# A convolution with per-image weights: the sums of an image read from PSUM by VectorE, its small steps gathered there, and the first eight pairs laid out anew

## The reference

```
x1 = group_norm(x)              # 32 groups of two neighbouring channels, eps 1e-5
pooled = x1.mean(pixels)
a = relu(fc1_w pooled + fc1_b)  # 4 values
att = softmax(fc2_w a + fc2_b)  # 4 values
agg_w = sum_k att[k] * weight[k]     # [64 out, 64 in, 3, 3] for each image
agg_b = att @ bias
out = x + conv3x3(x1, agg_w, pad 1) + agg_b
```

## Time and profile before

| | us |
|---|---|
| median of 3 runs | 323.28 (321.74 to 324.62) |
| the profiled execution | 323.93 |
| its span | 322.1 |
| TensorE busy | 301.2 |
| VectorE busy | 215.6 |
| ScalarE busy | 198.2 |
| GpSimd busy | 75.4 |
| mean granted clock of TensorE | 0.973 |

### The profile page before, as it was taken

The page is one execution under the profiler, slowest core; times in us unless marked ns, Lnnn a source line. Parts: engine busy times, 40 slices in busy tenths (PEclk is TensorE's granted clock), DMA queues, the critical chain, the costliest instruction groups (busy, mean ns, idle before and its releaser), DMA issues.

```text
span 322.1 us, 15578 instructions
## 1 busy us (share of the span) xinstructions
PE 301.2 (94%) x7038; PEld 265.2 (82%) x7038; DVE 215.6 (67%) x505; ACT 198.2 (62%) x260; POOL 75.4 (23%) x268
## 2 busy tenths in 40 slices
PE   7289877999899999999999999999999999999994
PEld 5157756988679999988999899967998799988883
DVE  2899584979569494948769494949678594719000
ACT  1090776786484849567684849486675849395321
POOL 1008266028310405040220404050311305000000
PEclk9769995999999999999999999999999999999999
DMA  7962306738392947648292947668392607051464
GB/s 260 421 268 65 141 2 150 254 86 286 77 275 93 228 177 176 227 112 288 51 258 111 239 166 184 218 136 273 84 293 56 180 2 205 2 147 60 118 171 119
DMA packets 16690, 53.61 MB, mean 166 GB/s; under 512 B 7280, under 2 KB 10352, under 8 KB 14704
## 3 DMA queue, kind: packets, MB, share of 16 engines
q1 hardware_dynamic: 16320, 52.40, 54.1%
q10 hardware_dynamic: 304, 0.22, 0.3%
HBM read 26.89 MB, written 25.69 MB: 163 GB/s over the span
## 4 chain that ended last, share of the span: by engine, by line
PE 82%; DVE 8%; POOL 4%; DMA 2%; issue 2%; ACT 0%; SPq 0%; POOLq 0%; DVEq 0%
PE acc L674 82%; DMA x<-x 2%; DVE stats L321 2%; DVE mix L402 2%; POOL var L285 1%; DVE wparts L337 1%; POOL vsum L281 1%; PE tiny L643 0%; DVE wl L446 0%; POOL root L286 0%; DVE mix L400 0%; DVE mv L329 0%; SPq L205 0%; POOL newton L287 0%; DVE o L511 0%
## 5 line engine op out<-in xcount | busy, mean ns | idle before, releaser
L581 ACT ACTIVATE o<-acc,out_par 128x392 f32<-128x392 f32 x127 | 78.9, 670 | 78.8 <-PE acc L674 78.4
L674 PE MATMUL acc<-xl,wh 64*64 64x385 f16 (+3 forms) x2304 | 119.8, 330 | 1.4 <-issue 1.4
L674 PE MATMUL acc<-xh,wh 64*64 64x385 f16 (+3 forms) x2304 | 118.1, 326 | 1.2 <-ACT wh L550 0.5
L674 PE MATMUL acc<-xh,wl 64*64 64x385 f16 (+3 forms) x2304 | 117.4, 325 | 0.6 <-issue 0.6
L674 PEld LDWEIGHTS acc<-xl,wh 64*64 64x64 f16 x2304 | 94.4, 109 | 11.4 <-issue 1.8
L674 PEld LDWEIGHTS acc<-xh,wl 64*64 64x64 f16 x2304 | 91.3, 107 | 11.3 <-issue 1.1
L674 PEld LDWEIGHTS acc<-xh,wh 64*64 64x64 f16 x2304 | 90.8, 108 | 11.9 <-ACT xh L532 0.9
L321 DVE BATCH_NORM_STATS2 stats<-x 128x6 f32<-128x448 f32 x112 | 60.8, 612 | 6.1 <-DMA x<-x 6.1
L455 DVE TENSOR_TENSOR xl<-x,xh 128x1568 f16<-128x1568 f32 x31 | 55.3, 1785 | 0.8 <-ACT x L520 0.8
L520 ACT ACTIVATE x<-x,xof,xsc 128x1568 f32<-128x1568 f32 x32 | 53.8, 1686 | 0.4
L527 ACT ACTIVATE xh<-x 128x1568 f16<-128x1568 f32 x28 | 42.0, 1502 | 0.4
(11 more groups left out here) (71 smaller groups left out, 146.3 us busy)
## 6 DMA issues: line engine op xcount, KB each, us to landing
x<-x SPq DMA_DIRECT2D x15, 1568.0 KB, 9.8
out<-o SPq DMA_DIRECT2D x30, 392.0 KB, 4.5
out<-o SPq DMA_DIRECT2D x30, 294.0 KB, 4.1
out<-o SPq DMA_DIRECT2D x44, 98.0 KB, 2.8
w_sb<-w_t SPq DMA_DIRECT2D x2, 576.0 KB, 8.7
out_par<-par SPq DMA_DIRECT2D x64, 0.5 KB, 2.1
x<-x SPq DMA_DIRECT2D x1, 896.0 KB, 7.1
x<-x SPq DMA_DIRECT2D x1, 448.0 KB, 3.7
```

Source lines behind the costliest of these rows:

```text
L581: nc.scalar.activation(o_sb[i][m][:, g * GN:(g + 1) * GN], acc[n % SLOTS][m][:, 0:GN], ACT.Identity, bias=out_par[i][m][:, 1:2], scale=out ...
L674: ins = nc.tensor.matmul(pixels[:, top:bottom, left:right], weights[i][halves[m], tap * C:(tap + 1) * C], window, start=start and step == ...
```

## The change

- Small steps. The group statistics of every pair run on VectorE (`group_stats` replaces `first_group_stats`, `first_scales` and GpSimd's chain). GpSimd keeps the root; a chunk of the next pair's statistics stands behind it on VectorE.
- Sums. `hidden`, the copies to `hid`, goes. VectorE reads `tiny` itself, which alternates between two banks by pair. The sums are asked for one pair ahead (not two), at places listed in `SUMS_AT`.
- Weights in another order. The second image's partitions hold the four sets as 2, 3, 0, 1, with bias and fc2 to match. So the first two sets of either half cover all four, and the largest is taken over one whole set and two halves of another.
- x in halves. x of pair 0 comes in five pieces, the weights are issued when the second has landed, x of pairs 1 to 3 when the first weights have; later x tiles come in two DMAs, on either side of `spread_params`. xh is made straight from x, in quarters for pairs 0 to 3 and in halves later; x is normalised afterwards. In pairs 1 to 7 VectorE normalises the first half.
- Orders. Pairs 0 to 3 mix, convert and multiply the weights in three parts of three taps. GpSimd makes the second low half of pairs 0 to 3. Pairs 0 to 7 take three groups by kind, then the fourth. The steps of `params` stand between those of the mixture. In pair 0 ScalarE makes the first share of two parts. The warming products are 36, 6 and 9.

The diff, cut to its core:

```diff
-TAP_ORDERS = ((4, 0, 1, 2, 3, 5, 6, 7, 8), (4, 6, 7, 8, 3, 5, 0, 1, 2))
+TAP_ORDERS = ((4, 3, 5, 0, 1, 2, 6, 7, 8), (4, 3, 5, 6, 7, 8, 0, 1, 2))
-PIECES = ((0, 1), (1, 3), (3, 7))
+PIECES = ((0, 1), (1, 3), (3, 5), (5, 6), (6, 7))
-WARM_PRODUCTS = (36, 10, 12)
-FIRST_TAPS = 5
+TURNED = (2, 3, 0, 1)
+WARM_PRODUCTS = (36, 6, 9)
+EARLY = 4
+GROUPED = 8
+SUMS_AT = ((1, 2, 3), (1, 2, 0), (1, 2, 0), (1, 2, 0), (1, 0, 6), (1, 0, 0), (0, 2, 6), (0, 2, 4), (0, 1, 0))
+SUMS_LATER = (1, 0, TAPS)
+LED = 7
+PART_ORDERS = (((0, 0), (0, 1), (0, 2), (1, 0), (1, 1), (1, 2), (2, 0), (2, 1), (2, 2)),
+               ((0, 0), (0, 1), (1, 0), (1, 1), (2, 0), (2, 1), (0, 2), (1, 2), (2, 2)))
...
 @block.sync
+            sp.wait_ge(x_piece[1], 16)
+            for n, ks in enumerate((slice(0, 1), slice(1, 2), slice(2, K))):
                 sp.dma_start(w_sb[:, ks, :], w_t[:, ks, :]).then_inc(s_weights[n], 16)
+            sp.wait_ge(s_weights[0], 16)
             for p in range(1, X_RING):
-                load(p)
+                for half in range(2):
+                    load(p, half)
             spread_params(0)
             for p in range(PAIRS - 1):
                 if p + X_RING < PAIRS:
-                    load(p + X_RING)
+                    load(p + X_RING, 0)
                 spread_params(p + 1)
+                if p + X_RING < PAIRS:
+                    load(p + X_RING, 1)
...
 @block.gpsimd
-            take_root()
-            low_inputs(0, 1)
-            for p in range(1, PAIRS):
-                group_stats(p)
+            for p in range(PAIRS):
+                take_root(p)
+                if p < EARLY:
+                    second_low_inputs(p)
...
 @block.vector
+            def group_stats(p):
...
+                if p == 0:
+                    largest_weights(0)
+                elif p + 1 < PAIRS:
+                    chunk_stats(p + 1, 0, 1)
+                dve.wait_ge(s_var, p + 1)
+                dve.wait_ge(s_root, p + 1)
...
             def logits(p):
-                dve.wait_ge(s_hid, 2 * (p + 1) + 2 * (p >= 1))
+                dve.wait_ge(s_fc1, 2 * (p + 1))
-                    out=prod[:], in0=hid[:, 0:K + 1].unsqueeze(1).to_broadcast([P, K, K + 1]), scalar=0.0, in1=fc2,
+                    out=prod[:], in0=tiny[p % 2][:, 0:K + 1].unsqueeze(1).to_broadcast([P, K, K + 1]), scalar=0.0,
...
+            def normalise(p, half):
+                nc.vector.tensor_scalar(v, v, xsc[i][:], xof[i][:], ALU.mult, ALU.add).then_inc(s_xn[half], 1)
...
+            for p in range(1, EARLY):
+                logits(p)
+                mixture_in_parts(p)
+                low_weights(p)
+                normalise(p, 0)
+                low_inputs(p, 0)
+                chunk_stats(p + 1, 1, CHUNKS)
+                channel_means(p + 1)
+                group_stats(p + 1)
+            for p in range(EARLY, PAIRS):
+                if p + 1 < PAIRS:
+                    chunk_stats(p + 1, 1, 2)
+                logits(p)
+                if p + 1 < PAIRS:
+                    chunk_stats(p + 1, 2, 3)
+                mixture(p)
+                if p + 1 < PAIRS:
+                    chunk_stats(p + 1, 3, 5)
+                low_weights(p)
+                if p <= LED:
+                    normalise(p, 0)
+                if p + 1 < PAIRS:
+                    chunk_stats(p + 1, 5, CHUNKS)
+                low_inputs(p, 0)
+                low_inputs(p, 1)
+                if p + 1 < PAIRS:
+                    channel_means(p + 1)
+                    group_stats(p + 1)
...
 @block.scalar
-            hidden(0)
+            high_quarter(0, 0)
             exponentials(0)
+            high_quarter(0, 2)
+            high_quarter(0, 1)
+            first_share(1)
+            first_share(2)
+            high_weights_part(0, 0)
+            high_quarter(0, 3)
+            high_weights_part(0, 1)
+            normalise_quarter(0, 0)
+            high_weights_part(0, 2)
+            for n in range(1, 4):
+                normalise_quarter(0, n)
+            for p in range(1, EARLY):
+                results(p - 1, 0)
+                results(p - 1, 1, (0,))
+                exponentials(p)
+                results(p - 1, 1, (1,))
+                high_quarter(p, 0)
+                high_quarter(p, 2)
+                results(p - 1, 2)
+                high_weights_part(p, 0)
+                high_quarter(p, 1)
+                high_weights_part(p, 1)
+                results(p - 1, 3)
+                high_weights_part(p, 2)
+                high_quarter(p, 3)
+                normalise_quarter(p, 2)
+                normalise_quarter(p, 3)
...
+                        high_from_x(p + 1, 0)
+                        exponentials(p + 1)
+                        results(p, 0)
+                        high_from_x(p + 1, 1)
+                        high_weights(p + 1)
+                        normalise(p + 1, 0)
+                        results(p, 1)
+                        normalise(p + 1, 1)
+                        results(p, 2)
...
 @block.tensor
+            def low(p, g, kind):
+                at = SUMS_AT[p] if p < len(SUMS_AT) else SUMS_LATER
+                if at[:2] == (kind, g) and p + 1 < PAIRS:
+                    products(p, g, weights, inputs, range(at[2]), stop=kind == 1)
+                    image_sums(p + 1)
+                    products(p, g, weights, inputs, range(at[2], TAPS), stop=kind == 1)
...
+            for p in range(GROUPED):
+                for n, g in PART_ORDERS[min(p, 1)] if p < EARLY else ():
+                    if n == 0:
+                        slot_free(p, g)
+                    if g == 0:
+                        pe.wait_ge(s_wh, mixed(p - 1) + n + 1)
+                    if (n, g) == (0, 0):
+                        pe.wait_ge(s_quarter[0], p + 1)
+                        pe.wait_ge(s_quarter[2], p + 1)
+                    elif (n, g) == (0, 1):
+                        pe.wait_ge(s_quarter[1], p + 1)
+                    elif (n, g) in ((2, 1), (0, 2)):
+                        pe.wait_ge(s_quarter[3], p + 1)
+                    high(p, g, range(3 * n, 3 * n + 3))
...
-        "w_t": np.tile(w.transpose(2, 0, 3, 1).reshape(C, K, TAPS * C), (2, 1, 1)),
+        "w_t": np.concatenate([w, w[:, turned]], axis=0),
```

More of the change, by code:

```diff
@@ new lines, in weight_scale @@
+                if p == 0:
+                    dve.wait_ge(s_range, 1)
+                    link(n + 5, nc.vector.scalar_tensor_tensor(
+                        out=wrange[:], in0=tiny[0][:, WEIGHTS:WEIGHTS + 1], scalar=total, in1=exsum[:],
+                        op0=ALU.add, op1=ALU.mult))
+                else:
+                    link(n + 5, nc.vector.tensor_scalar(wrange[:], total, exsum[:], None, ALU.mult))
+                nc.vector.reciprocal(wsc[i][:], wrange[:]).then_inc(s_wsc, 1)
@@ new lines, in share @@
+            def share(p, k, part, done):
+                columns = dict(out=mix[:, part], in0=w_sb[:, k, part])
+                if done > shares(p):
+                    dve.wait_ge(s_part, done)
+                if k == 0:
+                    ins = nc.vector.tensor_scalar(**columns, scalar1=ex[:, 0:1], scalar2=None, op0=ALU.mult)
+                else:
+                    ins = nc.vector.scalar_tensor_tensor(**columns, scalar=ex[:, k:k + 1], in1=mix[:, part],
+                                                         op0=ALU.mult, op1=ALU.add)
+                ins.then_inc(s_part, 1)
@@ L745, in _ @@
+            for p in range(GROUPED, PAIRS):
+                pe.wait_ge(s_wh, mixed(p))
+                for half in range(2):
+                    high_inputs_made(pe, p, half)
                 for g in range(GROUPS):
@@ L749, in _ @@
                         pe.wait_ge(s_wl, p + 1)
[L750 to L754 removed]
+                    low(p, g, 0)
+                    if g == 0:
+                        for half in range(2):
+                            pe.wait_ge(s_xl[half], p + 1)
+                    low(p, g, 1)
 def kernel(x, L0_conv_weight, L0_conv_bias, L0_conv_fc1_w, L0_conv_fc1_b, L0_conv_fc2_w, L0_conv_fc2_b):
```

521 lines of the change are left out of this document (242 added, 279 removed).

## The result

Four executions of the changed kernel took 313.99 us in the median (312.48 to 316.09); four of the kernel before, on the same chip, 323.78 (321.74 to 324.62). The ratio is 0.9704, with a 95% interval of 0.9651 to 0.9757: 3% less. The forecast was 317.9 (312.5 to 324). The profiled execution of after took 314.18 us with a span of 312.3; against before's 323.93 that is 9.8 us less, where the sum had 5.4.

A forecast was written before the change was run, and what follows sets the result against it. TensorE was taken to bound the kernel, with gains only ahead of 56 us. Terms -4.4 + 0.5 - 7.5 + 6.0 = -5.4 us took the profiled 323.93 to 318.5; the median, 0.65 lower, 317.9 us, range 312.5 to 324.

The forecast's parts named there:

- The start: Ahead of the first product: pair 0's statistics end at 8.3, first product from 20.86 to 16.5, -4.4 us.
- The bound of 9.3: End of pair 0's statistics if the last x piece lands no sooner and one chunk remains behind it.
- The clock: TensorE's granted clock around the first product: 0.9 us lost, between 0.2 and 2.6, against 0.4 now: +0.5 us.
- What goes: In the ramp, TensorE's waits of 0.8, 0.46 and 3.67 and 2.6 of half clock go: -7.5 us.
- What comes: New ramp stalls: 0.2 for pair 1's sums, 2.9 in pairs 1 to 3, 0.7 pair 4, 2.2 pairs 4 to 9: +6.0.
- Kept: TensorE time beyond the pairs' need, left unchanged: 2.3 us with no releaser (issue) and 1.7 of small joins.
- joins: The unnamed 1.7 us of TensorE's 12.0 beyond the pairs' need, taken as small and left as they are.
- A: Rival: the ramp's handovers are met, stalls of 2.5 us in place of 6.0, 314.4 us; chance 0.17.
- B: Rival: start gains less by late last piece (+1.0), late clock (+2.1) or stalls near 9 (+3): 320 to 323; chance 0.27.
- C: Rival: GpSimd is held by VectorE's two-input operations, TensorE waits 2 us in pairs 1 to 3: 323.9; chance 0.07.
- D: Rival: VectorE becomes the bound, 2.2 us more a pass, 0.8 lost in eleven pairs: 327; from 1.4 on; chance 0.07.
- At nothing: Items priced at zero: late pairs' slack, x halves, conversion from x, direct PSUM reads (-0.1 to +0.2 a pass), copies gone, tail.

The follow-up runs named there:

- run 3: Changed kernel with four whole maxima of the weights' quarters in the start, in place of one whole and two halves: 0.9742 of the kernel before.
- Run 2: Changed kernel without the two waits that hold back the weights and the later x tiles: 0.9696 of the kernel before.
- run 5: Changed kernel with the first x tile in three pieces in place of five: 0.9745 of the kernel before.
- run 6: Changed kernel with the first x tile in seven pieces of one chunk in place of five: 0.9707 of the kernel before.
- Run 1: Kernel before with only the group statistics of pairs 1 to 15 moved to VectorE, GpSimd keeping the root: 0.9845 of the kernel before.
- run 4: Changed kernel with VectorE instead of GpSimd making the second low halves of pairs 1 to 3: 0.9791 of the kernel before.
- run 9: Changed kernel with weights and inputs of pairs 1 to 3 prepared in wholes and halves, not parts and quarters: 0.9791 of the kernel before.
- run 12: Changed kernel with seven x pieces and 66 warming products in the first batch in place of 36: 313.72 us, 0.9704 of the kernel before.
- run 11: Changed kernel with five more chunk statistics, results unused, on VectorE in every pass from pair 8 on: 0.9891 of the kernel before.
- run 8: Changed kernel with a ScalarE copy of the sums from PSUM to SBUF, which VectorE then reads: 0.9877 of the kernel before.
- run 10: Changed kernel without the steps by which TensorE asks for the sums ever earlier in pairs 4 to 8: 0.9823 of the kernel before.

## Why the prediction was right, and where it was not

The direction, the range and the main mechanism (the waits for GpSimd's sums and the clock's dip behind them go) were right; the time came out 4 us lower than the forecast. The 4 us are a sum of errors of both signs, and part of the gain is not known to be the change's. Its terms, one by one:

**The start: -2.9 in the profiled execution, forecast -4.4.** Two parts. The chain behind the statistics, 9.94 before and 7.97 after, was forecast at 8.2: right, and run 3 shows the maxima's 1.2 us of it. The statistics end at 10.00, forecast 8.3: the mis-sized part. I let VectorE run through from 6.1, "since the bytes allow it", with x alone in the queues. It waited 1.74 us for the fourth and fifth chunk all the same. Run 2 shows nothing from holding back, run 5 that piece size matters. The bound of 9.3, "if the last piece lands no sooner than now", was the better reading: the nine kernels with five pieces end between 8.84 and 10.00, nearer to it than to 8.3.

**The clock: +0.5 forecast, +0.06 in the profiled execution** (0.46 lost, 0.4 before). The other kernels with the same warming lose 0 to 1.9 at the start: nothing in runs 5 and 6, below the lower bound of 0.2, and 0.5 to 1.9 in the rest. What sets the return was not found, so a term within 0.5 of the forecast is luck as much as reckoning.

**What goes: -7.5, right.** The sums' waits and the second dip of the clock are gone. Run 1 shows both gone with nothing else changed, though there 1.9 us of waits for low inputs and 1.4 for a slot came up in their place; the rest of the change keeps these away.

**What comes: +6.0 forecast, 2.9 measured** (4.9 of excess, less 0.5 of clock and 1.6 of gaps with no releaser). This is where the forecast missed most. Measured against 4.43 for a group, the high parts of pairs 1 to 4 cost 1.2, 0.4, 0.7 and 0.5 (forecast 1.3, 0.8, 0.8, 0.7): the reading of ScalarE's order as a strict queue was sound, and a little too strict. Its own times also make less than it took: third part 2.2 against 1.96, last quarter 3.1 against 2.45 and the 0.24 already waited, so 0.65 a pair and not 0.8. Pair 0's sums cost nothing (0.2 forecast; there 16.5 + 12.3 + 0.3 is 29.1, not 29.0). Behind pair 4's high part, pairs 4 to 9 cost 0.5 in all, one wait for low inputs in pair 8, against 2.2. (These parts make 3.3; pairs 0, 6 and 9 came out 0.1 shorter than 17.82 each.) That term was mis-sized at VectorE's pass. The passes of after, by the same step of each pair (pair 4 to 5, and 5 to 6):

```profile
86.62 0.15 DVE L396 TENSOR_TENSOR sums<-std,wbound 128x1 f32<-128x1 f32 x1
...
102.82 0.15 DVE L396 TENSOR_TENSOR sums<-std,wbound 128x1 f32<-128x1 f32 x1
...
119.74 0.15 DVE L396 TENSOR_TENSOR sums<-std,wbound 128x1 f32<-128x1 f32 x1
```

16.2 us, then 16.9, with a half normalised in each, where I had 17.3; and the normalising itself was under-rated:

```profile
L520 DVE TENSOR_SCALAR x<-x,xsc,xof 128x1568 f32<-128x1568 f32 x7 | 7.6, 1091 | 0.0
```

1.09 us against the 0.97 from the slope. The other steps must then be shorter than I summed them by about a microsecond: the small steps of the statistics, logits and scales overlap one another, starting 0.07 to 0.20 us apart. VectorE's busy time tells the same, 246.5 against the 255 to 265 forecast. In these two passes it won 1.6 and 0.9, not 0.5.

**Kept: 4.0 forecast (2.3 of issue and 1.7 of joins), 1.6 now.** That is two issue gaps, 0.36 and 0.65, with 0.29 each that the rows leave out. The "joins" were nothing that stays: they went with their waits. The gaps vary from none (runs 2, 4 and 9) to 3.0 us (run 12) between profiled executions of kernels that are nearly alike, and nothing here says why. So the 1.6 us that after has less of them than before are luck as far as is known.

Summed: the start is 1.5 dearer; the clock 0.4, the ramp 3.1 and the kept part 2.4 cheaper. That is -4.4, and -4.3 with the 0.1 us after the last product: the difference between 318.5 and 314.18.

**The rivals.** A (stalls of 2.5, 314.4 us) is nearest to the result: its price is what the ramp cost, within 0.4, and it had 0.17. That its time is met within half a us is luck: the start came 1.5 dearer, and the kept part made up for it. B did not come out as a sum, but the late landing, its first part, is what the profile shows. C did not happen: GpSimd's second low halves ran 3.17 us beside statistics with one input. Run 1's root at 28.81 shows that an operation which starts behind a two-input one of VectorE is held; the overlap of GpSimd's low half with such work was not tried. D did not happen, and run 11 moves its point from 1.4 us to about 2.3, by estimate.

**At nothing.** The direct reads of PSUM were priced right as operations: 173 ns for prod out of tiny, against 0.18 us in run 8 out of SBUF. Leaving out the copies was priced at nothing, and run 8 shows that in this kernel, with the copy behind the conversion, it is worth some 5 us (3.7 to 7.5 by the intervals): the hiding work that I named, the maxima, covers pair 0 alone. Run 8's split is partly open: 0.87 us a pass is read from the rows, 1.4 us is clock, the rest only follows from VectorE's lost lead.

## What to carry to other kernels

A small operation of another engine in a feedback path costs not its own 0.15 us but what stands in front of it in that engine's queue: here the reader waited 1.3 us and its pass grew by 0.9. Where the reader can take the data from where it lies, let it. Before trusting a sum over many small steps, take the pass from the repeating distance between two rows of one instruction, and count what the waits inside it can take up. Split the first load before holding other loads back; here five pieces did what seven do.

Before a gain is laid to a change, take out the gaps that have no releaser: here they were worth up to 3 us between kernels that are nearly alike.

## What the hardware showed that was not expected

- A two-input VectorE operation of 1.78 us on the same SBUF stretches a [128,1] GpSimd operation that starts 0.04 us behind it from 0.55 to 2.16 us (run 1). One that starts 0.01 us ahead of it stays at 0.55 (run 1), and so does one that starts behind a one-input statistic (after).
- TensorE's gap rows under-report by 0.29 us each in this kernel, since a 0.33 us matmul is followed by the next after 0.041 us.
- After waits of 1.4 (run 1) and 1.5 us (run 10) the granted clock stayed at 2.4 GHz. It fell to 1.2 within waits of 3.67 (before) and 2.16 us (run 11), and in run 5 1.1 us after work had resumed behind an issue gap of 1.9.
- Landings of x in five pieces differ by 1.2 us from one kernel to the next, and with the same warming the clock returned at the start between 16.8 (run 6) and 22.0 us (runs 3 and 8). Neither was explained.
